# Two graph-convolution layers on one core: one more short turn at the start, and other j-tiles summed by GpSimd

## The chip, the cores and the metric

The kernel runs on one core of a Trainium2 chip. The metric is the device time of one execution in microseconds. The profile is that of one execution.

## What is computed

```python
def _gcn_layer(x, adj, W, b):
    d_inv_sqrt = (jnp.sum(adj, axis=1) + 1e-09) ** (-0.5)
    msg = d_inv_sqrt[:, None] * adj * d_inv_sqrt[None, :] @ x
    return jax.nn.relu(msg @ W + b)
H_f = _gcn_layer(feature_x, adj, W_f, b_f)
H_s = _gcn_layer(spatial_x, adj, W_s, b_s)
attn = jax.nn.sigmoid(jnp.concatenate([H_f, H_s], axis=1) @ W_att + b_att)
x = _layernorm(x + attn * H_f + (1.0 - attn) * H_s)
```

`adj` is 4096 x 4096 in float32, 64 MiB; `x` and `spatial_x` are 4096 x 128. The two products of `adj` with the scaled features are nearly all the work, and each needs the row sums of `adj` first, since the features are scaled by the inverse square root of the degree.

## The kernel before

**Tiles.** The 4096 rows (i) are eight groups g of 512; the 4096 columns (j) are 32 j-tiles t of 128. A block is the transposed 128 x 512 piece of `adj` for one j-tile and one group. On the host the blocks are put in order, four to an item of 1 MiB, 64 items in all (0 to 63). The kernel brings item k into one of three buffers `raw`. ScalarE copies it into a rounded high part `Ah` (L720), VectorE subtracts that from `raw` for the low part `Al` (L533), and TensorE multiplies each block with the features Y of its j-tile, both features side by side as two halves, in three products (high by high, high by low, low by high): 3 x 2 x 4 = 24 matmuls of 512 columns per item.

**Y.** Y of tile t is x times the degree factor D of tile t. The sum of row r of i-tiles comes from `adj` in its natural layout, so every i-tile is loaded a second time: for i-tiles 0 to 23 in two halves of 1 MiB (`nat`, three buffers; the half number n is 2r or 2r + 1), summed by ScalarE (L730); GpSimd makes D (L828, L831), ScalarE the high part `Yh` (L747) and VectorE the low part `Yl` (L542). For i-tiles 24 to 31, which lie in groups 6 and 7 (`BY_COLUMN`), a part of the row is not loaded again: GpSimd adds up the blocks of these two groups as they pass through `raw` (`sum_block`, L870), for the j-tiles in `SUMMED`; after item 42 TensorE adds these over the partitions (`collect`), and `nat` brings only the remaining, plain columns.

**Runs and turns.** A run accumulates one group over a list of j-tiles in one of four PSUM pairs; a turn is four runs side by side, for one set of four groups. When a turn ends, VectorE adds its eight PSUM banks into `acc` (L550, L553: the evacuation). The function `plan` sets the turns: short ones at first, since Y of the next tile is not there yet (`[[0], [0, 1], [1, 2], [2, 3], [3, 4, 5]]`, by sets [0,1,2,3] and [4,6,5,7] in turn), then turns of four j-tiles, two old ones (`column`) and two fresh ones (`spread`), up to j-tile 23, and one last turn on 22 and 23. From item 48 on (`FINAL`) each group is finished over j-tiles 24 to 31, and the last layer follows group by group.

**What sets the order.** Each engine's program is written out over k. SyncE issues all loads from one queue: for item k first the halves in `parts[k]`, then an x load where `X_BEFORE` says so, then `raw` k, then an x load by `X_AFTER`. A load of `raw` k waits until item k - 3 has been subtracted (`low_ok`) and, where GpSimd sums blocks of it, until these sums are done (`block_sum_ok`); a load of half n waits for the sum of half n - 3. `parts` puts the halves 10, 11 with item 9, half n with item n - 2 for 12 to 29, n - 3 for 30 to 47, and the eight plain rows 48 to 55 in pairs with items 45 to 48. `pieces(k)` splits an item for ScalarE and VectorE: 1 + 1 + 2 blocks up to item 13, 2 + 2 up to `HALVED` (20), whole from there. Before `HALVED`, TensorE's first block of an item is taken in the order of `first_block`, which lets it begin before `Al` and `Yl` are whole. VectorE puts evacuations between its subtractions at set places (`evacuate_new`): some ahead of the first piece, some behind it, the rest at the item's end.

Of the kernel before, what the change touches and what calls it, by code (L numbers as in the profile page):

```python
# [11 lines left out]
P = 128  # L12
IB = 512
GT = 4
RAWS = 3
SPLITS = 3
NATS = 3
YRING = 8
ROWS = 12
STEPWISE = 14  # L20
HALVED = 20
WARM = [14, 8, 3]


def plan(T):

    G = T // GT
    FRONT = T - 2 * GT
    runs, items = [], []

    def add_runs(gs, tiles, pairs):  # L40
        new = [len(runs) + i for i in range(len(gs))]
        runs.extend((g, tiles, pair, (0, IB)) for g, pair in zip(gs, pairs))
        return new

    def column(new, tiles):
        blocks = [(e, t) for e in new for t in tiles]
        items.extend(blocks[i:i + 4] for i in range(0, len(blocks), 4))

    def spread(new, tiles):
        items.extend([(e, t) for e in new] for t in tiles)  # L50

    sets = [[0, 1, 2, 3], [4, 6, 5, 7]]
    for n, tiles in enumerate([[0], [0, 1], [1, 2], [2, 3], [3, 4, 5]]):
        spread(add_runs(sets[n % 2], tiles, range(4)), tiles)
    for n in range(3, FRONT // 2):
        old, fresh = [2 * n - 2, 2 * n - 1], [2 * n, 2 * n + 1]
        new = add_runs(sets[n % 2], old + fresh, range(4))
        column(new, old)
        spread(new, fresh)
    tiles = [FRONT - 2, FRONT - 1]  # L60
    column(add_runs(sets[0], tiles, [0, 1, 2, 0]), tiles)

    first = len(runs)
    s6, s7 = list(range(FRONT, FRONT + GT)), list(range(FRONT + GT, T))
    runs.extend((g, s6 + s7, (g + 1) % 3, (0, IB)) for g in range(G - 1))
    runs.append((G - 1, s6 + s7, 2, (0, IB // 2)))
    runs.append((G - 1, s6 + s7, 0, (IB // 2, IB)))
    order = [(0, s6), (1, s6), (0, s7), (1, s7)] + [(g, s) for g in range(2, G - 1) for s in (s6, s7)]
    order += [(G - 1, s6 + s7), (G, s6 + s7)]
    items.extend([(first + g, t) for t in s] for g, s in order)  # L70
    return runs, items


def build(nc, At, adj, xs_in, W_f, W_s, b_f, b_s, W_att, b_att, out):
# [51 lines left out]

    BY_COLUMN = [G - 2, G - 1]
    FULL = (G - 2) * GT
    SUMMED = range(5 * GT)
    PLAIN_FROM = len(SUMMED) * P  # L130
    parts = {k: [] for k in range(K)}
    parts[0], parts[2] = [0, 1], [2, 3]
    parts[4], parts[6], parts[8], parts[9] = [4, 5], [6, 7], [8, 9], [10, 11]
    for n in range(12, 30):
        parts[n - 2].append(n)
    for n in range(30, 2 * FULL):
        parts[n - 3].append(n)
# [61 lines left out]
    with ExitStack() as ctx:  # L199
# [122 lines left out]
            return bank, c * H2  # L322

        def nat_here(eng, n):
            eng.wait_ge(nat_in[n % NATS], 16 * (n // NATS + 1))

        def share_here(eng, i):
            eng.wait_ge(nat1_first if i == 1 else nat_in[SHARES[i][0]], 16)
# [7 lines left out]
        @block.sync  # L336
        def _(sp):
            def load_item(k):
                if k >= RAWS:
                    sp.wait_ge(low_ok, GT * (k - RAWS + 1))  # L340
                    if summed_blocks(k - RAWS):
                        sp.wait_ge(block_sum_ok, blocks_summed(k - RAWS))
                if k == 0:
                    sp.dma_start(raw[:, 0, 0:2 * IB], At_v[0, :, 0:2 * IB]).then_inc(raw0_in[0], 16)
                    sp.dma_start(raw[:, 0, 2 * IB:BLK], At_v[0, :, 2 * IB:BLK]).then_inc(raw0_in[1], 16)
                else:
                    sp.dma_start(raw[:, k % RAWS, :], At_v[k]).then_inc(raw_in[k % RAWS], 16)

            def load_part(n):
                r = tile_of(n)  # L350
                if n >= NATS:
                    part_summed(sp, n - NATS)
                if n == 1:
                    sp.dma_start(nat[:, 1, 0:N // 4], adj_v[0, 1, :, 0:N // 4]).then_inc(nat1_first, 16)
                    sp.dma_start(nat[:, 1, N // 4:N // 2], adj_v[0, 1, :, N // 4:N // 2]).then_inc(nat_in[1], 16)
                elif r < FULL:
                    sp.dma_start(nat[:, n % NATS, :], adj_v[r, n % 2]).then_inc(nat_in[n % NATS], 16)
                else:
                    sp.dma_start(nat[:, n % NATS, 0:N - PLAIN_FROM],
                                 adj_r[r, :, PLAIN_FROM:N]).then_inc(nat_in[n % NATS], 16)  # L360

            def load_x(m):
                sp.dma_start(xs[:, m * GT:(m + 1) * GT, :], xs_v[m]).then_inc(xs_sem[m], 16)

            def load_x_early(i):
                a, b = X_EARLY[i]
                c = a % GT
                sp.dma_start(xs[:, a:b, :], xs_v[a // GT, :, c:c + b - a, :]).then_inc(x_early[i], 16)

            for k in range(K):  # L370
                for n in parts[k]:
                    load_part(n)
                if k == 0:
                    load_x_early(0)
                if k in X_BEFORE:
                    load_x_early(X_BEFORE[k])
                load_item(k)
                if k in X_AFTER:
                    load_x(X_AFTER[k])
                if k == FINAL + 1:  # L380
                    sp.dma_start(Wfs[:, 0:H], W_f).then_inc(const_in, 16)
                    sp.dma_start(Wfs[:, H:H2], W_s).then_inc(const_in, 16)
                    sp.dma_start(bias[:, 0:H], bf_v).then_inc(const_in, 16)
                    sp.dma_start(bias[:, H:H2], bs_v).then_inc(const_in, 16)
                    sp.dma_start(watt[:, :], watt_v).then_inc(const_in, 16)
                    sp.dma_start(batt[:, :], batt_v).then_inc(const_in, 16)
            stores = [range(r, r + 2) for r in range(0, T - 2, 2)] + [range(T - 2, T - 1), range(T - 1, T)]
            for rows in stores:
                a, b = rows[0], rows[-1] + 1
                if b <= T - 2:  # L390
                    sp.wait_ge(norm_ok, b)
                else:
                    sp.wait_ge(last_norm_ok, b - (T - 2))
                sp.dma_start(out_p[:, a:b, :], xs[:, a:b, 0:F]).then_inc(stored, 16)
            sp.wait_ge(stored, 16 * len(stores))
# [131 lines left out]
        def _(dve):  # L527
# [118 lines left out]
            for k in range(K):  # L646
                ended = [e for e in evac_order if end_item[e] == k - 2]
                ending = [e for e in evac_order if end_item[e] == k - 1]
                if k < HALVED:
                    evacuate_new(ending[:2])  # L650
                else:
                    if len(ended) == GT:
                        evacuate_new(ended[:3])
                    if len(ending) == GT:
                        evacuate_new(ending[:1])
                for a, b in pieces(k):
                    low(k, a, b)
                    if a == 0:
                        if k >= HALVED and len(ending) == GT:
                            evacuate_new(ending[:2])  # L660
                        if k in (FINAL - 1, FINAL):
                            evacuate_new(ending[:1])
                        for r in y_at[k]:
                            y_low(r)
                        if STEPWISE <= k < HALVED:
                            evacuate_new(ending[:3])
                    elif a == 1:
                        evacuate_new(ending[:3])
                if k < HALVED or k in (FINAL - 1, FINAL):
                    evacuate_new(ending)  # L670
                if k == COLLECT + 2:
                    column_sums()
                mixing, joining = group_at(k, L_MIX), group_at(k, L_JOIN)
                if mixing is not None:
                    for r in of_group(mixing):
                        affine(r)
                if joining is not None:
                    for r in of_group(joining):
                        join(r)
                if mixing is not None:  # L680
                    for r in of_group(mixing):
                        logit(r)
                if k < K - 1:
                    evacuate_new(ended)
# [29 lines left out]
        def _(act):  # L714
# [11 lines left out]
            def row_sum(n):  # L726
                r = tile_of(n)
                nat_here(act, n)
                h, width = (n % 2, N // 2) if r < FULL else (0, N - PLAIN_FROM)
                act.activation(nat[:, n % NATS, 0:width], nat[:, n % NATS, 0:width], ACT.Copy,  # L730
                               accum_out=rs[:, r, h:h + 1]).then_inc(rs_act, 1)

# [236 lines left out]
```

## Time and profile before

| | us |
|---|---|
| median of 3 runs | 392.65 (392.58 to 392.72) |
| profiled execution | 392.9 |
| its span in the profile | 391.1 |
| TensorE busy | 376.7 (96%) |
| VectorE busy | 303.1 (78%) |
| ScalarE busy | 285.3 (73%) |
| GpSimd busy | 157.4 (40%) |
| data moved | 130.77 MB, 334 GB/s over the span |

A share of busy time is a mean over stages with different limits. The slices of the page show how the load moves over time; a timeline row gives the start, the length and, in brackets, the idle time ahead of it with what ended that.

### The profile page before, as it was taken

Reading aid. Unit: us, or ns where it says so; the run is one execution under the profiler, and the core shown is the slowest. Engines: PE = TensorE matmul, PEld = TensorE weight load, DVE = VectorE, ACT = ScalarE, POOL = GpSimd, SP = SyncE. Lnnn points to the kernel's source line nnn. Section 1 sums busy time; section 2 is a strip of 40 time slices with the busy share of each in tenths; the row PEclk is TensorE's granted clock in tenths of the full one; section 3 lists DMA queues with packets and bytes.
Section 4 is the critical chain, followed back from the end, with each engine's and each line's share of the span. In section 5 each row is a group of like instructions: output and inputs, shape, how many; then the busy total and the mean of one; then the engine's idle time right before and its main releaser. Section 6 shows DMA issues by size and latency. Waiting matters only on the chain. (4 is left out here: it accounts for less than half of the span.)

```text
span 391.1 us, 5491 instructions
## 1 busy us (share of the span) xinstructions
PE 376.7 (96%) x1778; PEld 312.8 (80%) x1778; DVE 303.1 (78%) x441; ACT 285.3 (73%) x379; POOL 157.4 (40%) x204
## 2 busy tenths in 40 slices
PE   7789999999999999999999999999999999999992
PEld 7567878788887788888888888888788888888992
DVE  2789996999576884879579593928976796889795
ACT  3677888788877887888878886778742666687656
POOL 2334512670065512771159200110100417877795
PEclk9999999999999999999999999999999999999998
DMA  8999999999999999999999999999675534455002
GB/s 272 421 418 423 421 419 415 424 418 418 422 416 422 421 421 418 421 419 421 421 420 422 421 416 421 415 408 386 250 271 211 213 108 152 172 159 165 4 25 81
DMA packets 24556, 130.77 MB, mean 334 GB/s; under 512 B 2640, under 2 KB 7632, under 8 KB 10448
## 3 DMA queue, kind: packets, MB, share of 16 engines
q1 hardware_dynamic: 24528, 130.43, 83.1%
q8 instruction: 14, 0.23, 0.2%
q14 instruction: 14, 0.11, 0.1%
HBM read 128.32 MB, written 2.10 MB: 333 GB/s over the span
## 5 line engine op out<-in xcount | busy, mean ns | idle before, releaser
L533 DVE TENSOR_TENSOR Al<-raw,Ah 128x2048 fp32r<-128x2048 f32 (+2 forms) x99 | 161.3, 1642 | 36.7 <-ACT Ah L720 36.6
L408 PE MATMUL sums<-Ah,Yh 128*128 128x512 f32 (+1 forms) x488 | 188.5, 386 | 1.2 <-DVE Al L533 1.0
L410 PE MATMUL sums<-Al,Yh 128*128 128x512 f32 (+1 forms) x488 | 186.6, 382 | 0.0
L409 PE MATMUL sums<-Ah,Yl 128*128 128x512 f32 (+1 forms) x488 | 186.6, 382 | 0.0
L720 ACT ACTIVATE Ah<-raw 128x2048 fp32r<-128x2048 f32 (+2 forms) x99 | 126.8, 1306 | 51.2 <-DMA raw<-in_At 31.9
L730 ACT ACTIVATE nat<-nat 128x2048 f32<-128x2048 f32 (+1 forms) x54 | 100.1, 1854 | 19.7 <-DMA nat<-in_adj 18.7
L408 PEld LDWEIGHTS sums<-Ah,Yh 128*128 128x128 f32 x488 | 91.7, 188 | 22.8 <-DVE Al L533 3.7
L410 PEld LDWEIGHTS sums<-Al,Yh 128*128 128x128 f32 x488 | 91.7, 188 | 18.0
L409 PEld LDWEIGHTS sums<-Ah,Yl 128*128 128x128 f32 x488 | 91.8, 188 | 17.1
L553 DVE TENSOR_TENSOR acc<-sums,acc 128x512 f32<-128x512 f32 (+1 forms) x122 | 77.1, 672 | 32.1 <-PE sums L410 29.5
L870 POOL TENSOR_TENSOR S<-S,raw 128x512 f32<-128x512 f32 x40 | 64.5, 1614 | 30.3 <-DMA raw<-in_At 27.2
L828 POOL TENSOR_SCALAR dg<-rs 128x1 f32<-128x1 f32 x23 | 14.4, 625 | 111.2 <-ACT nat L730 111.1
L876 POOL TENSOR_TENSOR fin<-fin 128x128 f32<-128x128 f32 x31 | 15.2, 490 | 32.1 <-ACT fin L754 32.0
L877 POOL TENSOR_TENSOR xs<-xs,fin 128x128 f32<-128x128 f32 x31 | 22.2, 715 | 0.0
L542 DVE SCALAR_TENSOR_TENSOR Yl<-xs,D,Yh 128x256 fp32r<-128x256 f32 x32 | 21.7, 693 | 0.2 <-ACT Yh L747 0.2
L763 ACT ACTIVATE fin<-xs,less 128x128 f32<-128x128 f32 x30 | 11.7, 389 | 13.8 <-POOL less L882 13.8
L597 DVE SCALAR_TENSOR_TENSOR xs<-fin,att,xs 128x128 f32<-128x128 f32 x30 | 11.9, 413 | 7.8 <-POOL xs L877 7.6
L754 ACT ACTIVATE fin<-nat 128x256 f32<-128x256 f32 x32 | 11.8, 410 | 8.1 <-DVE nat L567 8.0
L747 ACT ACTIVATE Yh<-xs,D 128x256 fp32r<-128x256 f32 x32 | 15.4, 496 | 3.0 <-POOL D L831 1.7
L441 PEld LDWEIGHTS sums<-Wfs,acc 128*128 128x128 f32 x128 | 15.6, 191 | 1.0 <-DVE acc L553 0.5
L441 PE MATMUL sums<-Wfs,acc 128*128 128x128 f32 x128 | 16.3, 276 | 0.1
L831 POOL TENSOR_TENSOR D<-dg,mhalf 128x1 f32<-128x1 f32 x23 | 14.7, 638 | 1.9
(56 smaller groups left out, 192.4 us busy)
## 6 DMA issues: line engine op xcount, KB each, us to landing
raw<-in_At SPq DMA_DIRECT2D x63, 1024.0 KB, 9.3
nat<-in_adj SPq DMA_DIRECT2D x47, 1024.0 KB, 11.6
nat<-in_adj SPq DMA_DIRECT2D x8, 768.0 KB, 9.6
xs<-in_xs SPq DMA_DIRECT2D x5, 512.0 KB, 10.5
out<-xs SPq DMA_DIRECT2D x15, 128.0 KB, 1.8
xs<-in_xs SPq DMA_DIRECT2D x5, 256.0 KB, 11.6
nat<-in_adj SPq DMA_DIRECT2D x2, 512.0 KB, 6.8
raw<-in_At SPq DMA_DIRECT2D x2, 512.0 KB, 8.7
```

Source lines behind the costliest of these rows:

```text
L408: pe.matmul(to, Yh[:, t % YRING, hs], high, start=first, stop=False)
L409: pe.matmul(to, Yl[:, t % YRING, hs], high, start=False, stop=False)
L410: mm = pe.matmul(to, Yh[:, t % YRING, hs], low, start=False, stop=last)
L441: return pe.matmul(sums[:, 3, bank, c + half * H:c + (half + 1) * H], acc[:, r // GT, half, q * P:(q + 1) * P], Wfs[:, half * H:(half + 1) ...
L533: dve.tensor_tensor(Al[:, k % SPLITS, a * IB:b * IB], raw[:, k % RAWS, a * IB:b * IB], Ah[:, k % SPLITS, a * IB:b * IB], ALU.subtract).the ...
L542: dve.scalar_tensor_tensor(out=Yl[:, r % YRING, :], in0=xs[:, r, :], scalar=D[:, r:r + 1], in1=Yh[:, r % YRING, :].bitcast(F32), op0=ALU.mult,
L553: dve.tensor_tensor(acc[:, g, half, a:b], sums[:, pair, half, 0:b - a], acc[:, g, half, a:b], ALU.add).then_inc(evac_ok, 1)
L720: act.activation(Ah[:, k % SPLITS, a * IB:b * IB], raw[:, k % RAWS, a * IB:b * IB], ACT.Copy).then_inc(high_ok, b - a)
L730: act.activation(nat[:, n % NATS, 0:width], nat[:, n % NATS, 0:width], ACT.Copy, accum_out=rs[:, r, h:h + 1]).then_inc(rs_act, 1)
L747: act.activation(Yh[:, r % YRING, :], xs[:, r, :], ACT.Copy, scale=D[:, r:r + 1]).then_inc(Yh_ok, 1)
L870: pool.tensor_tensor(S[:, g, :], S[:, g, :], raw[:, k % RAWS, j * IB:(j + 1) * IB], ALU.add).then_inc(block_sum_ok, 1)
L877: pool.tensor_tensor(xs[:, r, 0:F], xs[:, r, 0:F], f[:, H_S], ALU.add).then_inc(res_ok, 1)
```

## The change

The start gets one more turn of two items: j-tiles [3, 4], [4, 5], [5, 6, 7] in place of [3, 4, 5] and the turn [4, 5, 6, 7] behind it, so that there are 73 runs for 69. The sets of the later turns swap, so that groups 6 and 7 take j-tiles 20 and 21 in items 38 to 41 and not in 42 and 43. GpSimd sums j-tiles 4 to 21 in place of 0 to 19 (36 operations for 40), and the plain rows bring j-tiles 0 to 3 and 22 to 31, 14 for 12, each as two DMAs. Halves 10 and 11 go with item 10, 12 with 11, 13 with 12, 14 and 15 with 13. Items 20 and 21 are taken in two pieces, and in items that open a turn the third run's evacuation stands behind the second piece.

```diff
-HALVED = 20
+HALVED = 22
...
-    for n, tiles in enumerate([[0], [0, 1], [1, 2], [2, 3], [3, 4, 5]]):
+    for n, tiles in enumerate([[0], [0, 1], [1, 2], [2, 3], [3, 4], [4, 5], [5, 6, 7]]):
         spread(add_runs(sets[n % 2], tiles, range(4)), tiles)
-    for n in range(3, FRONT // 2):
+    for n in range(4, FRONT // 2):
         old, fresh = [2 * n - 2, 2 * n - 1], [2 * n, 2 * n + 1]
-        new = add_runs(sets[n % 2], old + fresh, range(4))
+        new = add_runs(sets[(n + 1) % 2], old + fresh, range(4))
...
-    column(add_runs(sets[0], tiles, [0, 1, 2, 0]), tiles)
+    column(add_runs(sets[1], tiles, [0, 1, 2, 0]), tiles)
...
-    SUMMED = range(5 * GT)
-    PLAIN_FROM = len(SUMMED) * P
+    SUMMED = range(4, 22)
+    PLAIN = [(0, SUMMED[0] * P), ((SUMMED[-1] + 1) * P, N)]
+    PLAIN_COLS = sum(b - a for a, b in PLAIN)
...
-    parts[4], parts[6], parts[8], parts[9] = [4, 5], [6, 7], [8, 9], [10, 11]
-    for n in range(12, 30):
+    parts[4], parts[6], parts[8], parts[10] = [4, 5], [6, 7], [8, 9], [10, 11]
+    parts[11], parts[12], parts[13] = [12], [13], [14, 15]
+    for n in range(16, 30):
...
-            eng.wait_ge(nat_in[n % NATS], 16 * (n // NATS + 1))
+            pieces_in = sum(len(PLAIN) if m >= 2 * FULL else 1 for m in range(n % NATS, n + 1, NATS))
+            eng.wait_ge(nat_in[n % NATS], 16 * pieces_in)
...
-                    sp.dma_start(nat[:, n % NATS, 0:N - PLAIN_FROM],
-                                 adj_r[r, :, PLAIN_FROM:N]).then_inc(nat_in[n % NATS], 16)
+                    c = 0
+                    for a, b in PLAIN:
+                        sp.dma_start(nat[:, n % NATS, c:c + b - a], adj_r[r, :, a:b]).then_inc(nat_in[n % NATS], 16)
+                        c += b - a
...
-                        if STEPWISE <= k < HALVED:
+                        if STEPWISE <= k < HALVED and items[k][0][0] != items[k][1][0]:
                             evacuate_new(ending[:3])
...
-                h, width = (n % 2, N // 2) if r < FULL else (0, N - PLAIN_FROM)
+                h, width = (n % 2, N // 2) if r < FULL else (0, PLAIN_COLS)
```

On SyncE's queue, from `raw` 8 to `raw` 13, before (a `nat` row is a half of an i-tile's row):

```order
L347 DMA raw<-in_At 128x2048
L357 DMA nat<-in_adj 128x2048 x2
L347 DMA raw<-in_At 128x2048
L357 DMA nat<-in_adj 128x2048
L347 DMA raw<-in_At 128x2048
L357 DMA nat<-in_adj 128x2048
L368 DMA xs<-in_xs 128x512
L347 DMA raw<-in_At 128x2048
L357 DMA nat<-in_adj 128x2048
L347 DMA raw<-in_At 128x2048
L357 DMA nat<-in_adj 128x2048
L347 DMA raw<-in_At 128x2048
```

And now:

```order
L350 DMA raw<-in_At 128x2048 x2
L360 DMA nat<-in_adj 128x2048 x2
L350 DMA raw<-in_At 128x2048
L360 DMA nat<-in_adj 128x2048
L350 DMA raw<-in_At 128x2048
L360 DMA nat<-in_adj 128x2048
L373 DMA xs<-in_xs 128x512
L350 DMA raw<-in_At 128x2048
L360 DMA nat<-in_adj 128x2048 x2
L350 DMA raw<-in_At 128x2048
```

`raw` 9 now stands directly behind `raw` 8, ahead of the halves 10 and 11; the halves 14 and 15 stand together ahead of `raw` 13, where the two orders meet again; the x load for j-tiles 6 and 7 goes with item 12, not 11.

On the same queue, from `raw` 47 to `raw` 49, with the plain rows 54 and 55 between, before:

```order
L347 DMA raw<-in_At 128x2048
L359 DMA nat<-in_adj 128x1536 x2
L347 DMA raw<-in_At 128x2048 x2
```

And now:

```order
L350 DMA raw<-in_At 128x2048
L364 DMA nat<-in_adj 128x512
L364 DMA nat<-in_adj 128x1280
L364 DMA nat<-in_adj 128x512
L364 DMA nat<-in_adj 128x1280
L350 DMA raw<-in_At 128x2048 x2
```

Each plain row is two DMAs, 1792 columns in place of 1536; the same holds ahead of `raw` 45, 46 and 47.

On VectorE, from the last piece of item 7 to the second pieces of item 9, before:

```order
L533 TENSOR_TENSOR Al<-raw,Ah 128x1024
L553 TENSOR_TENSOR acc<-sums,acc 128x512 x2
L533 TENSOR_TENSOR Al<-raw,Ah 128x512
L542 SCALAR_TENSOR_TENSOR Yl<-xs,D,Yh 128x256
L533 TENSOR_TENSOR Al<-raw,Ah 128x512
L533 TENSOR_TENSOR Al<-raw,Ah 128x1024
L533 TENSOR_TENSOR Al<-raw,Ah 128x512
L542 SCALAR_TENSOR_TENSOR Yl<-xs,D,Yh 128x256
L533 TENSOR_TENSOR Al<-raw,Ah 128x512
```

And now:

```order
L538 TENSOR_TENSOR Al<-raw,Ah 128x1024
L558 TENSOR_TENSOR acc<-sums,acc 128x512 x2
L538 TENSOR_TENSOR Al<-raw,Ah 128x512
L547 SCALAR_TENSOR_TENSOR Yl<-xs,D,Yh 128x256
L538 TENSOR_TENSOR Al<-raw,Ah 128x512
L538 TENSOR_TENSOR Al<-raw,Ah 128x1024
L558 TENSOR_TENSOR acc<-sums,acc 128x512 x4
L538 TENSOR_TENSOR Al<-raw,Ah 128x512 x2
L558 TENSOR_TENSOR acc<-sums,acc 128x512 x2
```

The evacuation of the turn [3, 4] stands in item 9, four operations ahead of its first piece, two behind the second and two at its end; the same again in item 11 for the turn [4, 5].

## Rows read from the trace of the kernel before

**Rows 1.** Page slices; windows (last columns: clock, DMA share, GB/s)
```profile
DVE  2789996999576884879579593928976796889795
POOL 2334512670065512771159200110100417877795
DMA  8999999999999999999999999999675534455002
...
2.00:275.00 273.00, 268.07 (x1194) 219.28 (x1195) 209.19 (x225) 213.82 (x226) 96.90 (x96) 1.00 1.01 415
245.00:275.00 30.00, 30.00 (x142) 25.06 (x141) 21.16 (x25) 23.56 (x28) 3.08 (x7) 1.00 1.01 401
```

**Rows 2.** TensorE timeline (start, length): first matmuls of items 0, 8, 22, 27, 48
```profile
12.43 0.47 PE L424 MATMUL sums<-Ah,Yh 128*128 128x512 f32 x1 [2.46 <-ACT Yh L747]
...
59.20 0.39 PE L424 MATMUL sums<-Ah,Yh 128*128 128x512 f32 x1
...
137.35 0.39 PE L408 MATMUL sums<-Ah,Yh 128*128 128x512 f32 x1
...
164.55 0.40 PE L408 MATMUL sums<-Ah,Yh 128*128 128x512 f32 x1
...
280.38 0.39 PE L410 MATMUL sums<-Al,Yh 128*128 128x512 f32 x1
280.80 0.47 PE L408 MATMUL sums<-Ah,Yh 128*128 128x512 f32 x1
```

**Rows 3.** Timeline of ScalarE: row sums, copies of raw 47 and 48
```profile
257.05 1.49 ACT L730 ACTIVATE nat<-nat 128x1536 f32<-128x1536 f32 x1 [1.16 <-DMA nat<-in_adj]
...
258.92 1.49 ACT L730 ACTIVATE nat<-nat 128x1536 f32<-128x1536 f32 x1 [0.29 <-DMA nat<-in_adj]
...
267.74 1.92 ACT L720 ACTIVATE Ah<-raw 128x2048 fp32r<-128x2048 f32 x1 [0.99 <-DMA raw<-in_At]
...
272.62 1.48 ACT L730 ACTIVATE nat<-nat 128x1536 f32<-128x1536 f32 x1
...
274.44 1.92 ACT L720 ACTIVATE Ah<-raw 128x2048 fp32r<-128x2048 f32 x1 [0.26 <-DMA raw<-in_At]
```

**Rows 4.** Timeline of VectorE, from item 47's subtraction to item 48's
```profile
271.05 2.28 DVE L533 TENSOR_TENSOR Al<-raw,Ah 128x2048 fp32r<-128x2048 f32 x1
273.25 1.28 DVE L553 TENSOR_TENSOR acc<-sums,acc 128x512 f32<-128x512 f32 x2
274.45 1.66 DVE L542 SCALAR_TENSOR_TENSOR Yl<-xs,D,Yh 128x256 fp32r<-128x256 f32 x4
276.03 2.47 DVE L553 TENSOR_TENSOR acc<-sums,acc 128x512 f32<-128x512 f32 x4
278.42 2.28 DVE L533 TENSOR_TENSOR Al<-raw,Ah 128x2048 fp32r<-128x2048 f32 x1
```

**Rows 5.** Two loads in SyncE's timeline, then each one's time to landing
```profile
78.99 0.43 SPq L357 DMA_DIRECT2D nat<-in_adj  x1
79.46 0.43 SPq L368 DMA_DIRECT2D xs<-in_xs  x1
...
DMA to landing us min/median/max: 11.5/11.5/11.5
...
DMA to landing us min/median/max: 11.7/11.7/11.7
```

**Rows 6.** Timelines of ScalarE and VectorE: copy and subtraction for item 27
```profile
159.49 1.92 ACT L720 ACTIVATE Ah<-raw 128x2048 fp32r<-128x2048 f32 x1 [0.57 <-DMA raw<-in_At]
...
161.54 2.79 DVE L533 TENSOR_TENSOR Al<-raw,Ah 128x2048 fp32r<-128x2048 f32 x1 [1.03 <-ACT Ah L720]
```

**Rows 7.** Page group of GpSimd's sums; timelines of VectorE and GpSimd
```profile
L870 POOL TENSOR_TENSOR S<-S,raw 128x512 f32<-128x512 f32 x40 | 64.5, 1614 | 30.3 <-DMA raw<-in_At 27.2
...
114.99 2.07 DVE L533 TENSOR_TENSOR Al<-raw,Ah 128x1024 fp32r<-128x1024 f32 x1
...
114.68 3.52 POOL L870 TENSOR_TENSOR S<-S,raw 128x512 f32<-128x512 f32 x2
```

## Prediction, made before the changed kernel was run

> **What bounds the kernel now.** I read the load share first, then TensorE's order of time, then the two places where TensorE and the loads come close.
>
> The page's row of slices shows the DMA engines at nine tenths or more from the second slice to the 27th, and the window from 2 to 275 us has a DMA share of 1.01 at 415 GB/s [rows 1]. Until about 275 us there is no gap in the loads. So the moment at which a load lands is set by the bytes queued ahead of it, not by when its buffer came free. This is the row to see: a buffer freed earlier, or TensorE arriving earlier, lands nothing sooner.
>
> TensorE looks full too. An item is 24 matmuls. Five items, 27 to 31 say, start one after the other: item 22 begins at 137.35 us and item 27 at 164.55 us [rows 2], so 27.20 / 5 = 5.44 us per item with no wait. Against that step, items 0 to 7 took 59.20 - 12.43 = 46.77 us, 3.25 more than 8 x 5.44, and items 8 to 21 took 137.35 - 59.20 = 78.15 us, 1.99 more than 14 x 5.44 [rows 2]. These 5.24 us are all that the front can give. Afterwards only crumbs of wait are left, the largest at item 48: its first matmul starts 0.42 us after the one before, where 0.23 is the step [rows 2], so 0.19 us.
>
> At item 48 (the first on j-tiles 24 to 27) three chains meet. ScalarE starts its copy of raw 48 at 274.44 us, held 0.26 us by the load [rows 3]; VectorE works without a break from 271.05 us and starts the subtraction for item 48 at 278.42 us [rows 4]; TensorE starts at 280.80 us. From item 49 on the loads have room (the DMA row falls to 6, 7, 5 tenths [rows 1]), and TensorE runs without waits for data, so what item 48 loses the end loses.
>
> **The change, part by part.**
>
> *More bytes before raw 48.* Each of the eight rows of i-tiles 24 to 31 now brings 14 j-tiles instead of 12: 896 KB for 768 KB, in all 8 x 128 KB = 1.05 MB, all queued ahead of raw 48. A 768 KB load costs 258.92 - 257.05 = 1.87 us from one to the next [rows 3]; by bytes alone the new one costs 1.87 x 14 / 12 = 2.18 us, +0.31. But it comes as two DMAs, 256 KB in rows of 2 KB and 640 KB in rows of 5 KB. The nearest row for the first is an x load of 256 KB with rows of 2 KB: the load before it, issued at 78.99, lands 11.5 us later, at 90.49; it, issued at 79.46, lands 11.7 us later, at 91.16, so 0.67 us [rows 5]. The second by bytes is 1.87 x 640 / 768 = 1.56. Together 2.23 us, +0.36. Over eight: 2.5 to 2.9 us. I take 2.8, since the 2 KB row is a measured one. Raw 48 then lands at 274.4 + 2.8 = 277.2, and raw 47 (six of the eight ahead of it) at 267.7 + 2.1 = 269.8 us.
>
> The Trainium skill (SBUF — State Buffer, Summary: rules for kernel authors) says of a transfer-bound load "one DMA, not several", and its page DMA: Bandwidth & Descriptors (Anatomy of one DMA) fits a fixed cost of about 2.0 us to a DMA on the GpSimd path; if eight more DMAs each paid that in line, the result would be an estimate of 16 us more, near 409.5. The trace speaks against it for queued loads, since the 256 KB load adds only 0.67 us.
>
> *What follows at item 48.* From the start of ScalarE's copy to VectorE's subtraction it takes 161.54 - 159.49 = 2.05 us where nothing else is in the way [rows 6], and from the subtraction to TensorE 280.80 - 278.42 = 2.38 us: 4.43 us. The copy at 277.2 gives TensorE 281.65. VectorE's own chain gives the same: the subtraction for item 47 cannot start before 269.8 + 2.05 = 271.85, the work from it to the next subtraction is 278.42 - 271.05 = 7.37 us in a row [rows 4], so 279.2, and + 2.38 = 281.6. So item 48 starts 0.85 us later than now, between 0.55 (2.5 us of bytes) and 1.0 (2.9). ScalarE's longer row sums (1.48 us x 14 / 12 = 1.73) fit before it: raw 48 is later by more than they grow.
>
> *The added turn.* Turns [3,4], [4,5], [5,6,7] stand for [3,4,5] and its follower, so four runs more are evacuated: 8 operations; a row of four takes 2.47 us [rows 4], so 4.9 us of VectorE, in items 8 to 11. VectorE is at nine tenths in slices 4 to 6, about 29 to 59 us, where turns of two items already are, and at 6 to 9 behind them [rows 1]. The row of nines belongs to the stretch in which TensorE ran only 3.25 us behind its step, most of it before item 4; so a two-item turn fits, barely. Lower bound 0; upper bound 4.9 us exposed. I take 0.5 us.
>
> *Row loads later.* The halves 10 to 14 are queued one item later, so raw 9 has two loads of 1 MB fewer ahead of it, raw 10 to 12 one fewer. That relieves items 9 to 12. From raw 13 on the bytes ahead are what they were.
>
> *GpSimd.* Sums over j-tiles 0 to 3 go: eight operations of 1.61 us [rows 7], in items 1, 2, 5 and 6. A half-item subtraction beside such sums took 2.07 us where the whole one takes 2.28 [rows 4, 7]. So VectorE gets back about 1 us per item there. Tiles 20 and 21 are summed instead, in items 40 and 41; two sums are 3.2 us, less than the 4.43 us of copy and subtraction, so the buffer isn't held longer. *Halves up to item 21*: worth up to 1.1 us of earlier start at items 20 and 21 (half of 2.28).
>
> *What the front can keep.* TensorE may reach item 22 up to 2 us earlier. But raw 27 has the same bytes ahead as before. Its copy starts at 159.49, so item 27 cannot start before 159.49 + 4.43 = 163.9, against 164.55 [rows 2, 6]: at most 0.6 us survives, and item 48, late by its load, takes that too. What is late next is thus raw 48, whatever the front does.
>
> **Sum.** The profiled execution is 392.9 us, span 391.1 and 1.8 around it, 0.25 above the median of the runs. +0.85 gives 393.75 in its terms and 393.5 for the median. A measurement of this kernel can tell about 0.2%, 0.79 us, from no change, so this forecast lies at the border.
>
> **The rivals.**
>
> *A, the forecast: the load of item 48 sets the end.* 393.5, from 393.1 to 393.9. For it: a DMA share of 1.01 throughout.
>
> *B, not slower: the loads have slack that the shares hide.* From 245 to 275 us only 401 GB/s moved, against 415 over the whole stretch [rows 1]; over 30 us that is 30 x 14 / 415 = 1.0 us of lag. A part of it is seen: raw 48's copy starts 6.70 us after raw 47's, where bytes ask for 2 x 1.87 + 2.5 = 6.2 [rows 3]. If this lag does not come again, raw 48 lands at 276.2, TensorE can start item 48 at 280.65, and it gets there in time because of the front: 0.15 us better than now, 392.5. It decides as soon as the lag shrinks by 0.85 us. Against it: nothing in the change touches what causes the lag. More than 0.6 us is not to be gained in any case, for raw 27 caps it: 392.05.
>
> *C, VectorE loses more in the front.* If the 4.9 us of evacuations lie bare between items 8 and 13, less the 2.0 us of waits that disappear there, TensorE is 2.9 us late: 395.5. It counts only beyond the 1 us that item 48 waits anyway. For it: the nines in slices 4 to 6, and GpSimd's sums now meeting a two-item turn in items 9 and 10. By the Trainium skill (SBUF — State Buffer, Who interferes with whom) a VectorE operation with two SBUF inputs and a GpSimd one that reads SBUF exclude each other for the whole instruction; four sums of 1.61 us would be an estimate of 6.4 us more blocked, for 397 at worst. The 2.07 us row agrees in kind, not in full size. Against C: items 5 and 6 are such a turn now and cost TensorE little.
>
> *D, the change does not do what it says.* If the sums of tiles 20 and 21 came too late for their collection after item 42, TensorE would wait there; GpSimd's row in the page has slack in that stretch [rows 1, 7].
>
> **How the numbers follow.** A 0.67, B 0.13, C 0.17, D 0.03. A is split at 0.79 us: 0.38 slower, 0.29 the same. B is the same but for 0.03 that I leave to a gain beyond the cap. C and D are slower but for 0.02. So faster 0.03, same 0.41, slower 0.56. The range runs from 392.2, between B and the cap, to 395.0, within C; about 1 in 8 is left out.
>
> **What would show it.** ScalarE's copy of raw 48 at 277 to 277.5 us, with an idle time put down to the load; item 48 on TensorE near 281.6 and a wait of some 1.5 us ahead of it, more than now; the end following it. The front: less wait in items 1 to 12 and TensorE ahead by 1 to 2 us at item 22, 0.6 at item 27. The whole is wrong if raw 48 lands before 276.5, if TensorE reaches item 48 later than 281.6 by itself, or if the DMA share falls below 1 before 270 us.

## The result: slower by 0.47%, at the upper part of the range

The changed kernel takes 394.57 us (median of 6 runs, 393.98 to 395.67) against 392.73 us (6 runs, 392.58 to 393.05) for the kernel before beside it: a ratio of 1.0047, interval 1.0037 to 1.0057. The forecast was 393.5 with a range of 392.2 to 395.0, and slower was its likeliest verdict. Sign and range held, but the loss is 1.84 us where 0.85 was worked out, and 394.57 lies above the 393.1 to 393.9 that rival A, the forecast proper, allowed for.

In the rows PE is TensorE, ACT ScalarE, DVE VectorE and POOL GpSimd. The profiled execution took 394.39 us with a span of 392.6, 1.5 more than the 391.1 of before. The page of the changed kernel, slices of VectorE, GpSimd and DMA as in [rows 1], and GpSimd's sums, which answer to [rows 7]:

```profile
span 392.6 us, 5517 instructions
...
DVE  2788999979794888659686696828986796879895
POOL 2000126216810464126901793010100417877795
DMA  7999999999999999999999999999775524445012
...
L875 POOL TENSOR_TENSOR S<-S,raw 128x512 f32<-128x512 f32 x36 | 61.8, 1717 | 21.2 <-DMA raw<-in_At 18.3
```

The nines of the DMA row end with slice 28 in both kernels; the slice behind them shows 7 where it showed 6, which is where the extra megabyte shows. The 36 sums take 1717 ns each on average where 40 took 1614.

ScalarE of the changed kernel, from the last row sums ahead of raw 47 to the copy of raw 48 (the answer to [rows 3]):

```profile
265.34 1.71 ACT L735 ACTIVATE nat<-nat 128x1792 f32<-128x1792 f32 x1 [0.25 <-DMA nat<-in_adj]
...
267.60 1.71 ACT L735 ACTIVATE nat<-nat 128x1792 f32<-128x1792 f32 x1 [0.47 <-DMA nat<-in_adj]
...
270.20 1.92 ACT L725 ACTIVATE Ah<-raw 128x2048 fp32r<-128x2048 f32 x1 [0.80 <-DMA raw<-in_At]
272.02 1.69 ACT L752 ACTIVATE Yh<-xs,D 128x256 fp32r<-128x256 f32 x4
273.62 1.69 ACT L735 ACTIVATE nat<-nat 128x1792 f32<-128x1792 f32 x1
...
275.30 1.69 ACT L735 ACTIVATE nat<-nat 128x1792 f32<-128x1792 f32 x1
...
277.16 1.92 ACT L725 ACTIVATE Ah<-raw 128x2048 fp32r<-128x2048 f32 x1
```

Its VectorE over the same items (the answer to [rows 4]), and TensorE at item 48 (the answer to the last of [rows 2]):

```profile
272.25 2.30 DVE L538 TENSOR_TENSOR Al<-raw,Ah 128x2048 fp32r<-128x2048 f32 x1 [1.01 <-ACT Ah L725]
274.46 1.28 DVE L558 TENSOR_TENSOR acc<-sums,acc 128x512 f32<-128x512 f32 x2
275.66 1.67 DVE L547 SCALAR_TENSOR_TENSOR Yl<-xs,D,Yh 128x256 fp32r<-128x256 f32 x4
277.24 2.48 DVE L558 TENSOR_TENSOR acc<-sums,acc 128x512 f32<-128x512 f32 x4
279.64 2.28 DVE L538 TENSOR_TENSOR Al<-raw,Ah 128x2048 fp32r<-128x2048 f32 x1
```

```profile
281.23 0.39 PE L415 MATMUL sums<-Al,Yh 128*128 128x512 f32 x1
...
282.02 0.47 PE L413 MATMUL sums<-Ah,Yh 128*128 128x512 f32 x1 [0.41 <-issue]
```

Read them from the bottom. Item 48 starts at 282.02 instead of 280.80, 1.22 us late. VectorE's subtraction stands 2.38 us ahead of it, as before, at 279.64. Ahead of that VectorE runs in one row back to 272.25, where it waited 1.01 us for ScalarE's copy of raw 47, and that copy waited 0.80 us for its load. So the load of item **47** set the time. The copy of raw 48 starts at 277.16 without an idle time put down to its load: ScalarE's own row, now 6.96 us from copy to copy (6.70 before, [rows 3]), ended as late as the load, which landed at 277.01. And it wasn't this copy that VectorE's subtraction waited for: by the 2.05 us of [rows 6] it could have started at 279.21, 0.43 us before it did.

### The profile page after: what moved, and what is told of

Same layout as the page of the kernel before. It is cut to its first block and busy times, and to the rows that moved or that the text cites. A ratio compares the mean times of both kernels' runs of the same rounds, so it can differ in the third digit from the quotient of the medians.

```text
span 392.6 us, 5517 instructions
## 1 busy us (share of the span) xinstructions
PE 378.5 (96%) x1778; PEld 314.5 (80%) x1778; DVE 308.3 (79%) x451; ACT 287.1 (73%) x381; POOL 153.9 (39%) x200
## 5 line engine op out<-in xcount | busy, mean ns | idle before, releaser
L735 ACT ACTIVATE nat<-nat 128x2048 f32<-128x2048 f32 (+1 forms) x54 | 101.8, 1886 | 21.7 <-DMA nat<-in_adj 21.0
L558 DVE TENSOR_TENSOR acc<-sums,acc 128x512 f32<-128x512 f32 (+1 forms) x130 | 81.9, 673 | 25.3 <-PE sums L415 23.1
L875 POOL TENSOR_TENSOR S<-S,raw 128x512 f32<-128x512 f32 x36 | 61.8, 1717 | 21.2 <-DMA raw<-in_At 18.3
L833 POOL TENSOR_SCALAR dg<-rs 128x1 f32<-128x1 f32 x23 | 15.5, 673 | 124.5 <-ACT nat L735 124.2
L429 PE MATMUL sums<-Ah,Yh 128*128 128x512 f32 x44 | 13.9, 398 | 2.5 <-ACT Yh L752 2.5
```

What stands on the lines that cost most here:

```text
L558: dve.tensor_tensor(acc[:, g, half, a:b], sums[:, pair, half, 0:b - a], acc[:, g, half, a:b], ALU.add).then_inc(evac_ok, 1)
L833: pool.tensor_scalar(dg[:, r:r + 1], rs[:, r, 0:1], rs[:, r, 1:2], 1e-9, ALU.add, ALU.add).then_inc(dg_ok, 1)
L875: pool.tensor_tensor(S[:, g, :], S[:, g, :], raw[:, k % RAWS, j * IB:(j + 1) * IB], ALU.add).then_inc(block_sum_ok, 1)
```

## The experiments

All medians are set against runs of the kernel before on the same chip (392.73 to 392.86 us); the experiments ran on several chips. The ratios and their intervals are those on record; they are not the quotient of the two medians and differ from it by up to 0.0006. Times inside a kernel are from its profiled execution.

### Bytes and the split, apart

In the kernel before, 14 j-tiles in one DMA a row, nothing else:

```diff
-    SUMMED = range(5 * GT)
+    SUMMED = range(18)
```

> The kernel before with one edit: GpSimd sums j-tiles 0 to 17, the plain rows bring 14 j-tiles as one DMA of 896 KB. Nothing else of the change. Theory L (loads ahead of raw 48 set the loss): 8 x 0.31 = 2.5 us more ahead of raw 48, its copy starts at 276.9, TensorE starts item 48 at 276.9 + 4.43 = 281.3 to 281.6, so 0.5 to 0.8 us slower, ratio 1.0013 to 1.002. Rival V (the added turn on VectorE sets it): no difference, ratio 1.000.

393.37 us (11 runs, 393.22 to 393.56), 1.0016, interval 1.0007 to 1.0025. Then in the kernel before the same bytes as two DMAs a row:

```diff
-    SUMMED = range(5 * GT)
+    SUMMED = range(2, 20)
+    PLAIN = [(0, SUMMED[0] * P), ((SUMMED[-1] + 1) * P, N)]
...
+                    for a, b in PLAIN:
+                        sp.dma_start(nat[:, n % NATS, c:c + b - a], adj_r[r, :, a:b]).then_inc(nat_in[n % NATS], 16)
+                        c += b - a
```

> The kernel before, GpSimd sums j-tiles 2 to 19, the plain rows bring the same 14 j-tiles' worth as two DMAs (256 columns, then 1536). Against the run with one DMA of the same bytes this is the price of the split. Theory L, with the price of short rows: 0.05 to 0.1 us a row, 0.4 to 0.8 us more than the run with one DMA, ratio 1.002 to 1.004. Rival: the split costs nothing, the same ratio as with one DMA (1.0013 to 1.002). Rival V: 1.000.

394.12 us (5 runs, 393.85 to 394.37), 1.0034, interval 1.0021 to 1.0046. This kernel splits a row into 256 and 1536 columns, where the change splits it into 512 and 1280, and it differs from the one above also in that GpSimd sums tiles 18 and 19 and not 0 and 1. TensorE at item 48, first with one DMA a row, then with two:

```profile
281.28 0.47 PE L408 MATMUL sums<-Ah,Yh 128*128 128x512 f32 x1 [0.40 <-issue]
```

```profile
282.25 0.47 PE L412 MATMUL sums<-Ah,Yh 128*128 128x512 f32 x1 [0.42 <-issue]
```

Item 48 is 0.48 and 1.45 us late, and the spans are 391.6 and 392.6. The old front with the new loads thus gives the whole span of the changed kernel, and 1.36 of the 1.84 us of the medians. The bytes cost 0.6 us of the median and the split (with the two other sums) 0.75 more.

How much of this lies in the queue is seen by the time from the landing of raw 36 (205.5 to 206.2 us in all of them, the same bytes being queued ahead of it) to that of raw 47 and raw 48. The profile gives the time to landing in tenths, so each entry is good to about 0.1:

| kernel | raw 36 to raw 47 | raw 36 to raw 48 |
|---|---|---|
| before | 61.99 | 68.74 |
| 14 j-tiles, one DMA a row | 63.79 (+1.80) | 70.62 (+1.88) |
| 14 j-tiles, two DMAs a row | 64.15 (+2.16) | 71.06 (+2.32) |
| the change without the sums of two tiles (below) | 64.11 (+2.12) | 71.09 (+2.35) |
| the change | 64.66 (+2.67) | 71.55 (+2.81) |
| the change, another execution | 64.69 (+2.70) | 71.67 (+2.93) |

One DMA a row costs +1.80 for the six rows ahead of raw 47, 0.30 each, which is the 0.31 of the bytes. Two cost 0.35 to 0.45 each. In the second kernel of this section another 0.6 us had arisen before raw 36, where the queue holds the same loads: 0.4 of it in one half behind raw 28, which took 3.45 us where it takes 3.04 in the first. That part isn't the split. But its profiled run (394.37) is only 0.25 us above its median, so of the 0.75 us by which the medians differ the queue shows 0.36 at raw 47, and the rest isn't located.

### The new front without the new loads

The changed kernel with its plain rows back at 12 j-tiles in one DMA, so that what is left of the change is the added turn, the swapped sets, the moved halves, and pieces up to item 21 (the sums over tiles 0 to 3 are back too):

```diff
-    SUMMED = range(4, 22)
-    PLAIN = [(0, SUMMED[0] * P), ((SUMMED[-1] + 1) * P, N)]
+    SUMMED = range(20)
+    PLAIN = [((SUMMED[-1] + 1) * P, N)]
```

> The changed kernel, but GpSimd sums j-tiles 0 to 19 and the plain rows bring 12 j-tiles in one DMA, as before: the front turn, the swapped sets, the later halves and the two pieces stay. Theory L: raw 48 lands as before (274.4), TensorE is 0.6 us ahead from item 27 on and nothing takes it back: 0.3 to 0.6 us faster than before, ratio 0.9985 to 0.9992. Rival V (added turn and the sums met by it): slower than before by 0.8 to 1.8 us, ratio 1.002 to 1.005.

392.93 us (11 runs, 392.81 to 393.65), 1.0008, interval 0.9999 to 1.0017. Item 48 starts at 280.64, 0.16 earlier than before, and the span is the same 391.1. Neither expectation came true: this front costs at most 0.17%, by the interval, and gives nothing. It is not quite the front of the change. Its TensorE reaches item 22 at 137.00, the changed kernel's at 135.50 (135.55 in another execution) and the kernel before's at 137.35. The one edit between the first two that touches items before 22 is the sums over tiles 0 to 3, which the change doesn't make, and all eight traces with the changed front divide by it: item 22 starts at 135.50 to 135.82 in the three without these sums and at 136.57 to 137.00 in the five with them. So some 1 us of the front's lead came from GpSimd doing less, and not from the added turn.

Then with fewer bytes than before, 10 j-tiles in one DMA (`SUMMED = range(22)`):

> The changed kernel, but GpSimd sums j-tiles 0 to 21 (44 operations) and the plain rows bring 10 j-tiles in one DMA: 1.05 MB less ahead of raw 48 than before, 2.1 MB less than in the changed kernel. Theory L: raw 48 lands near 272 us and holds nobody; what is left is the cap at raw 27, so 0.4 to 0.6 us faster than before, ratio 0.9985 to 0.999, and a narrow spread of the runs. Rival V: slower than before, and slower than the variant with 12 j-tiles because of four more sums.

393.64 us (392.74 to 394.18), 1.0018, interval 1.0009 to 1.0027: slower with less to load, although its profiled execution (392.76, item 48 at 280.48) is not. So the expected gain of 0.4 to 0.6 us did not come. Its executions differ by 1.4 us. Another profiled execution took 393.31, and there TensorE was past the collection behind item 42 at 253.54 and not at 252.94:

> The changed kernel with 10 plain j-tiles once more, unchanged, for the profile of another execution: its runs lay between 392.74 and 394.18, and the profile at hand is of the fastest kind. Theory G: in one above 393.5 TensorE waits for VectorE in items 38 to 42 by 0.5 to 1 us. Rival: the wait is elsewhere, in the front or the last layer.

There TensorE waited 0.26 us for VectorE at item 39 (0.5 to 1 us was expected of an execution above 393.5, which this isn't) and some 0.4 at item 27.

What this kernel shares with the change, and the one with 12 j-tiles does not, is the sums of tiles 20 and 21 in items 40 and 41; groups 6 and 7 take only tiles 18 and 19 in items 38 and 39. GpSimd's four sums of these tiles and then VectorE's subtractions for items 39, 40 and 41 in the changed kernel:

```profile
226.32 1.29 POOL L875 TENSOR_TENSOR S<-S,raw 128x512 f32<-128x512 f32 x1
227.76 3.15 POOL L875 TENSOR_TENSOR S<-S,raw 128x512 f32<-128x512 f32 x1
231.05 3.26 POOL L875 TENSOR_TENSOR S<-S,raw 128x512 f32<-128x512 f32 x1
234.45 1.29 POOL L875 TENSOR_TENSOR S<-S,raw 128x512 f32<-128x512 f32 x1
```

```profile
226.66 3.10 DVE L538 TENSOR_TENSOR Al<-raw,Ah 128x2048 fp32r<-128x2048 f32 x1
...
230.88 2.27 DVE L538 TENSOR_TENSOR Al<-raw,Ah 128x2048 fp32r<-128x2048 f32 x1
...
234.52 3.38 DVE L538 TENSOR_TENSOR Al<-raw,Ah 128x2048 fp32r<-128x2048 f32 x1
```

A sum with nothing beside it takes 1.29 us, a subtraction 2.27. Whichever starts while the other runs takes longer by what is left of the other, less some 0.13 us. The subtraction at 226.66 finds a sum that ends at 227.61, 0.95 later: 3.10 is 2.27 + 0.83. The one at 234.52 finds 1.22 left: 3.38 is 2.27 + 1.11. The sum at 227.76 finds 2.00 us of subtraction left: 3.15 is 1.29 + 1.86. All 30 subtractions of the kernel before and the changed one that took over 0.15 us longer than their fellows fit this to 0.02 us. The mean of 1614 ns [rows 7] thus mixes 1.29 with sums that waited:

```profile
L870 POOL TENSOR_TENSOR S<-S,raw x40: 1287/1299/3393, 15.0 to 213.6; 128x512 f32<-128x512 f32 x40
```

The kernel before has such a row of four sums too, at 207.42 in items 36 and 37, and a subtraction of 3.08 us beside it. What is new is where it stands. The buffers are held longer, and raw 44 is issued at 237.92, where the kernel before has 234.95. The next two kernels leave the sums of tiles 20 and 21 out of the computation, first with 10 j-tiles in the plain rows, then with the change's own loads. The edit of the second is:

```diff
-    SUMMED = range(4, 22)
-    PLAIN = [(0, SUMMED[0] * P), ((SUMMED[-1] + 1) * P, N)]
+    SUMMED = range(4, 20)
+    PLAIN = [(0, 4 * P), (22 * P, N)]
```

> The changed kernel with 10 plain j-tiles in one DMA, and GpSimd sums only j-tiles 0 to 19: the sums over j-tiles 20 and 21 are left out of the computation (the degrees of rows 3072 to 4095 lack them), so that GpSimd does nothing in items 40 and 41. Its twin with these sums took 393.64 us with runs from 392.74 to 394.18. Theory G (what made that one slow and uneven is GpSimd's sums in items 38 to 41, beside VectorE, which has no slack there): 392.3 to 392.8 us, spread under 0.5 us. Rival (something in the loads or the front, alike in both): 393.6 us again, with the same spread.

> The changed kernel with all its loads (14 plain j-tiles in two DMAs, 1792 columns summed by ScalarE), but the sums over j-tiles 20 and 21 left out of the computation. Theory G with theory L: the load's part of the loss stays, as in the kernel before with two DMAs (394.12 us, 1.0034), less what the front gives, and GpSimd's part goes: 393.6 to 394.1 us, spread under 0.6 us, against 394.57 us and a spread of 1.7 us in the changed kernel. Rival (loads alone): 394.5 us, spread as there.

With 10 j-tiles: 393.09 (392.88 to 394.14), 1.0012, interval 1.0003 to 1.0021, 0.5 below the 393.64 with the sums. With the change's loads: 394.22 (5 runs, 394.05 to 395.29), 1.004, interval 1.0028 to 1.0053, so 0.35 below the changed kernel; its item 48 starts at 281.68. Both lie above what was expected, and neither spread is as narrow as expected. Its subtraction for item 39, which had taken 3.10, takes 2.27 again:

```profile
226.72 2.27 DVE L538 TENSOR_TENSOR Al<-raw,Ah 128x2048 fp32r<-128x2048 f32 x1
```

By the medians the sums cost 0.35 to 0.5 us, but in both pairs the intervals overlap and the two kernels ran on different chips, so this isn't clear of the noise. Nor are they all of the unevenness: 5 of the 11 runs with 10 j-tiles stay above 393.4. In the profiles of the two kernels with the change's loads the sums make TensorE wait 0.23 us more at item 39, and it is past the collection at 253.43 with them, at 253.15 without. This does not reach item 48, since ahead of it VectorE waits 1.01 us for the copy of raw 47. And the buffers that they hold delay no load: raw 44, issued at 237.92 with them and at 235.02 without, landed between 247.5 and 247.6 in both, and raw 45 at 254.5 in both.

The swap of the sets, in the kernel before:

```diff
-    sets = [[0, 1, 2, 3], [4, 6, 5, 7]]
+    sets = [[4, 6, 5, 7], [0, 1, 2, 3]]
...
-                raw_here(pool, k)
+                raw_here(pool, k, j)
...
-            for k in range(1, FINAL):
+            for k in range(FINAL):
```

The last two pairs of lines let GpSimd sum blocks in item 0, where groups 6 and 7 now come first.

> The kernel before with the two sets of groups swapped from the first turn on and nothing else: turns, sums over j-tiles 0 to 19, loads and their sizes are before's; GpSimd's last sums fall in items 38 and 39. Theory S (the uneven runs and some 0.2 us in the last layer come with the swapped sets, through GpSimd's sums beside VectorE): 392.9 to 393.3 us, some of the runs above 393.4. Rival (they come with the added turn): as before, 392.8 us, no run above 393.3.

393.20 us, 1.0006, interval 0.9998 to 1.0015, but from 392.21 to 393.74 in 11 runs. The interval doesn't exclude no difference, and the spread of 1.5 us comes with the swap. Which stretch the longer executions lose it in is open, since none of the changed kernel's above 394.6 was profiled. A repeat of the changed kernel gave 394.59, with item 48 at 282.31 and a wait of 1.07 us ahead of item 27. VectorE waited 1.07 us for the copy of raw 47 there, and raw 48 landed at 277.4, so it shows the same loss again and not that of the longest executions:

> The changed kernel once more, unchanged, for the profile of another execution: its runs lay between 393.98 and 395.67, and the profile at hand is of one at 394.39. If an execution above 395 is caught, its trace tells where the further 1 us goes. Theory G (GpSimd's sums beside VectorE): a wait of TensorE for VectorE's subtraction in items 38 to 42. Rival (loads): raw 48 lands later than 277.0.

### Where the front's gain goes

The changed kernel at item 27 (TensorE), the row that answers to 164.55 in [rows 2]:

```profile
162.85 0.39 PE L415 MATMUL sums<-Al,Yh 128*128 128x512 f32 x1
164.03 0.50 PE L413 MATMUL sums<-Ah,Yh 128*128 128x512 f32 x1 [0.79 <-DVE Al L538]
```

TensorE arrived 0.95 us before it could go on, having been at item 22 at 135.50, 1.85 us ahead of the kernel before. The cap can be lifted: the halves 30 to 39 are queued one item later each, so that raw 27 has fewer bytes ahead. First on the new front with 12 j-tiles:

```diff
-    for n in range(16, 30):
+    for n in range(16, 40):
...
-    for n in range(30, 2 * FULL):
+    for n in range(40, 2 * FULL):
```

> The changed front with 12 plain j-tiles (sums over 0 to 19), and the halves 30 to 39 also go with item n - 2, not n - 3, so that raw 27 to raw 36 each have one load of 1 MB fewer ahead. Theory C (raw 27 caps what the front gives): the 0.6 us cap is lifted to some 3 us, and up to 1.5 us show: 391.5 to 392.5 us, ratio 0.9965 to 0.9995. Rival (VectorE and not the load of raw 27 keeps TensorE): the same as with the cap, 392.9 us.

392.46 us (392.11 to 393.66), 0.9994, interval 0.9985 to 1.0003, which doesn't exclude no gain. Item 48 starts at 280.15, 0.49 earlier than in the same front with the cap. But that isn't the cap's doing alone: the profile with the cap has no wait at item 27, where TensorE came at 164.20, just after the subtraction ended, and 0.32 of the 0.49 us stood already at item 22 (136.68 for 137.00), ahead of the moved halves. Then the same on the kernel before, whose TensorE isn't early at item 27 (`range(12, 30)` becomes `range(12, 40)`):

> The kernel before, with the halves 30 to 39 moved one item later in the same way and nothing else. Theory C: before's TensorE is 0.6 us from that cap and would gain nothing from lifting it, 392.7 us, ratio 1.000; only with the changed front would it pay. Rival: the cap binds in some executions already, 0.3 us faster.

392.95 us, 1.0005, interval 0.9996 to 1.0013: alone it gives nothing. In its profile TensorE still waits 0.50 and 0.41 us more than a step in items 20 and 21. So the last kernel takes the kernel before with just two things, the pieces up to item 21 (with the rule for evacuations that goes with them) and the later halves, and none of the turns, sets, sums and rows of the change:

```diff
-HALVED = 20
+HALVED = 22
...
-    for n in range(12, 30):
+    for n in range(12, 40):
...
-    for n in range(30, 2 * FULL):
+    for n in range(40, 2 * FULL):
...
-                        if STEPWISE <= k < HALVED:
+                        if STEPWISE <= k < HALVED and items[k][0][0] != items[k][1][0]:
```

> The kernel before with its own turns, sets and sums; from the change only the two-piece items 20 and 21 (and the evacuation rule that goes with them), and besides the halves 30 to 39 one item later, so that raw 27 does not cap. In before with later halves TensorE waits 0.9 us in items 20 and 21. Theory P (these waits come from taking the items whole; the added turn and swapped sets are not needed): they go, item 48 starts 0.6 to 0.9 us earlier, 391.9 to 392.3 us, ratio 0.998 to 0.999. Rival (VectorE or the load of raw 20 holds them just as well in pieces): 392.8 us, ratio 1.000.

392.13 us (11 runs, 391.88 to 392.87) against 392.83, 0.9982, interval 0.9973 to 0.9991: **faster than both kernels**. Its ScalarE at the copies of raw 47 and 48, its VectorE at item 47, and its TensorE at item 48:

```profile
268.32 1.92 ACT L720 ACTIVATE Ah<-raw 128x2048 fp32r<-128x2048 f32 x1 [1.07 <-DMA raw<-in_At]
...
274.68 1.91 ACT L720 ACTIVATE Ah<-raw 128x2048 fp32r<-128x2048 f32 x1
```

```profile
270.37 2.29 DVE L533 TENSOR_TENSOR Al<-raw,Ah 128x2048 fp32r<-128x2048 f32 x1 [0.27 <-ACT Ah L720]
```

```profile
280.15 0.47 PE L408 MATMUL sums<-Ah,Yh 128*128 128x512 f32 x1 [0.38 <-issue]
```

TensorE waits for nothing from item 18 to item 42, starts item 27 at 163.49, which is earlier than the cap would let it, and is past the collection at 252.24, 1.07 us earlier than before. At item 48 0.65 of it is left. The first matmul there starts 0.54 us more than a step late, and VectorE waited for the copy of raw 47, whose load had come late: the last loads are the bound again. The pieces without the later halves were not run, so how much of the gain needs both isn't known.

## Point by point: why it was slower, and why by more than forecast

**Right: the loads set the end.** The step "a buffer freed earlier, or TensorE arriving earlier, lands nothing sooner" carried the case: with and without the sums in items 40 and 41 raw 44 was issued 2.9 us apart and landed at the same time. Raw 48 landed at 277.01, where 277.2 was forecast (+2.64 for +2.8; from raw 36 on it is +2.81). The old front with the new loads has the same span of 392.6 as the whole change.

**Right: the cap at raw 27.** Item 27 "cannot start before 163.9"; it started at 164.03. TensorE was ahead by 1.85 us at item 22 (1 to 2 forecast) and by 0.52 at item 27 (0.6 forecast), and only the kernels with the halves moved started item 27 before 163.9.

**Mis-sized: raw 47, the term that counted.** Six rows were put at 0.35 each, +2.1 (269.8); from raw 36 to raw 47 it was +2.67, and raw 47 landed at 270.12, +2.50. The prediction had both chains, through raw 48 and through VectorE from raw 47, at 281.6. The second came out longer: 272.25 + 7.39 + 2.38 = 282.02. That is 0.4 of the 0.65 us missing in the profile. With the same loads but without the sums of two tiles raw 47 is +2.12 from raw 36 on, and item 48 starts at 281.68, the forecast's 281.65. So the term is right for the loads alone, and short by half a microsecond in the whole change, in both of its profiled executions. Most of the difference arose between raw 45 (254.5 with the sums and without) and raw 46 (263.1 for 262.8), some 19 us after the last sum; with one profile of the kernel without them, whether the sums or scatter made it stays open. The working had a scatter in it that it didn't use: before, the two rows between raw 47 and raw 48 landed 0.5 us late by bytes. This is the lag of rival B. It did not come again, so these rows cost only 0.1 to 0.2 in all, while the six ahead paid more than their bytes. So B's mechanism was real and worth 0.5 us, but at a load that no longer was the bound. Of the wait of some 1.5 us forecast ahead of item 48 TensorE shows 0.57, and 0.58 more at 278.58, where an evacuation behind the late subtraction of item 47 held it; the copy of raw 48 shows none of the idle time forecast for it.

**Mis-sized: the split.** With one DMA a row the loss is 0.6 us of the median, with two 1.35. I had put the split at 0.05 us a row; over the six rows ahead of raw 47 it took 0.05 to 0.15 a row, 0.3 to 0.9 us in all. The Trainium skill (SBUF — State Buffer, Summary: rules for kernel authors) says "one DMA, not several" of a transfer-bound load: right in direction, and here more than half of the loads' loss. Far from the 2.0 us a DMA that was weighed, though.

**Failed: "two sums are 3.2 us, less than the 4.43 us ..., so the buffer isn't held longer".** The sums ran beside whole-item subtractions and waited for them, so that the four took 9.4 us and raw 44 was issued 3 us later. The step is wrong, but it cost the loads nothing up to raw 45, and what it cost in the end, 0.35 to 0.5 us by the medians, isn't clear of the noise. The 1.61 us was a mean over sums that took 1.29 us and sums that waited. That the two engines keep each other out was weighed for items 9 and 10 alone and not for items 40 and 41, and the 2.07 us row was taken as agreeing "in kind, not in full size". It agrees in full size: the half-item subtraction takes 1.21 us by itself, it started at 114.99, and the first of the two sums, begun at 114.68, had 0.98 us left. The Trainium skill (SBUF — State Buffer, Who interferes with whom) calls the ports that the two engines share an exclusive lock. The trace agrees, but for some 0.13 us of overlap; the delay is what is left of the other's instruction, and only as long as the whole of it if both start at once.

**By luck in the range.** The sum's own bounds for its mechanism were 393.1 to 393.9. The range went up to 395.0 for the sake of rival C, a front that costs more, and that rival fell. So the measured 394.57 is inside for another reason than the one that the room was left for.

**Unforeseen: 0.2 us behind item 48.** From its first matmul to the end of the span the kernel before and its five variants take 110.3 to 110.4 us, the eight traces with the changed front 110.5 to 110.6. The variants hold the swapped sets, the pieces up to item 21, the later halves and both forms of the loads, so it is none of these alone; what it is stays open.

**The scatter.** The profile has +1.5, the medians +1.84. The changed kernel's profiled run is 0.18 below its median, and that of before 0.17 above.

**The rivals.** C, a dearer front, fell: 392.93 with the new front alone, at most 0.17% above before, and in the change TensorE is ahead at item 22. The 4.9 us of added evacuations cost nothing measurable. D fell too: the profile shows no wait at the collection beyond that of before.

## What to carry to other kernels

Where a load queue never runs empty, price a change by the bytes and the DMAs ahead of each load that something waits for, and follow every such load, not the last one alone: two chains that meet at one time need an error bar each. Work given to an idle GpSimd isn't free if VectorE streams the same stretch: price each meeting at what is left of the one that runs. And take a bundle apart: of this one the pieces up to item 21, together with later halves that the change did not have, pay 0.7 us, while the added and split loads cost 1.4.

## What the runs showed of the hardware that I had not expected

- A single load lands about 1 us behind its bytes, once between raw 36 and raw 47, and not at the same one in every kernel: in the kernel before the second plain row took 2.83 us instead of 1.87, with one DMA of 14 j-tiles the same row 3.14 instead of 2.18, in the changed kernel it was a half some 12 us earlier, 3.47 instead of 2.47. It isn't a matter of chance where: in all eight traces with the changed front that same half is late, at 238.7 to 239.0 us, and in the five with the old front and the old order of the sets one of the first two plain rows, at 250.1 to 252.7.
- Eight loads of 896 KB, each split in two, cost 0.4 to 1.0 us more in the queue than unsplit, some 0.1 us each (+2.32 to +2.93 for +1.88 at raw 48).
- A VectorE subtraction with both inputs in SBUF and a GpSimd sum keep each other out: whichever starts second takes longer by what is left of the first, less 0.13 us (3.10 and 3.38 us for 2.27; 3.15 and 3.26 for 1.29). An evacuation, which reads one side from PSUM, isn't held: two of them beside the sum at 227.76 took 1.27 us, where two with no sum beside them take 1.28.
- The first matmuls ran at a lower granted clock in some executions. In the changed kernel TensorE stood idle for 2.45 us, began item 0 at 12.24, and was granted 0.63 of full speed from 12 to 14 us and 0.52 from 14 to 16, so mostly the lower of its two levels, 1.2 GHz for 2.4. Its matmuls start 0.43 us apart until 15.96 us and 0.23 from there on, at a granted 1.00, and the page shows an 8 in the clock row of that slice. The kernel before was granted 1.00 throughout, and so was the repeat of the changed kernel after an idle time of 2.37 us. The 1.6 us lost were made up by item 4: the kernel before waits 2.5 us for data in items 1 to 3, the changed one doesn't.
- Kernels with swapped sets spread over 0.8 to 1.7 us from run to run. The kernel before spreads over 0.4 to 0.9 us, beside them on the same chips, and the last one over 0.4 but for a single run. I have no cause for it.
